# Mixer's head in a four-stage transformer kernel: one convolution tap moved to ScalarE and GpSimd, a logarithm as a polynomial, GpSimd's work in another order

## The reference

```
zxbcdt = LN(x) @ in_proj_w.T                      # z 512, xBC 640, dt 4 columns
dt     = softplus(zxbcdt[..., -4:] + dt_bias)     # 4 heads
xBC    = silu(conv(xBC, 4 taps, causal))          # per channel, along the tokens
xs, B, C = xBC[:512], xBC[512:576], xBC[576:640]
y      = ssd(xs * dt, -exp(A_log) * dt, B, C)     # state-space scan in chunks
y      = (y + xs * D) * silu(z)
x     += (y * rsqrt(mean(y * y) + 1e-5) * norm_w) @ out_proj_w.T
```

## Time and profile before

| | |
|---|---|
| three runs | 520.99, 521.13, 521.2 us, median 521.13 |
| the profiled execution | 521.09 us, of which the span from the first to the last instruction is 519.3 |
| granted TensorE clock, mean | 0.999 of full speed |
| busy: PE, DVE, ACT, POOL | 503.5, 406.6, 313.2, 145.6 us |
| mixer's head, from the first x_resid to the last convolution tap | about 321 to 348.6 us |
| mixer's loop, from decays(0) | about 346 to 402 us |

### The profile page before, as it was taken

The page is one execution under the profiler, slowest core; times in us unless marked ns, Lnnn a source line. Parts: engine busy times, 40 slices in busy tenths (PEclk is TensorE's granted clock), DMA queues, the critical chain, the costliest instruction groups (busy, mean ns, idle before and its releaser), DMA issues.

```text
span 519.3 us, 9035 instructions
## 1 busy us (share of the span) xinstructions
PE 503.5 (97%) x2950; PEld 426.7 (82%) x2951; DVE 406.6 (78%) x895; ACT 313.2 (60%) x784; POOL 145.6 (28%) x285
## 2 busy tenths in 40 slices
PE   6999999999999999999999999989999999999996
PEld 5778899999999988678888888867989768888885
DVE  5736567667666789899999899985888879899777
ACT  4656878688687754574534445899873365344342
POOL 1432434345243320020110111379554020020110
PEclk9999999999999999999999999999999999999999
DMA  7320100000000303100030000000000000000101
GB/s 278 125 81 3 40 2 2 1 1 2 2 2 8 151 2 107 42 1 1 0 141 2 2 0 1 1 2 1 1 2 1 0 1 1 1 0 1 40 2 40
DMA packets 5933, 14.17 MB, mean 27 GB/s; under 512 B 640, under 2 KB 3200, under 8 KB 5888
## 3 DMA queue, kind: packets, MB, share of 16 engines
q1 hardware_dynamic: 5888, 13.60, 7.5%
HBM read 12.55 MB, written 1.05 MB: 26 GB/s over the span
## 4 chain that ended last, share of the span: by engine, by line
PE 79%; DVE 12%; issue 3%; ACT 3%; DMA 1%; POOL 1%; SPq 0%; DVEq 0%; ACTq 0%; POOLq 0%
PE psum L172 61%; PE psum L493 4%; DVE xs L1994 2%; PE psum L525 2%; PE psum L1809 1%; PE psum L241 1%; DMA w_raw<-in_wk 1%; PE psum L1813 1%; PE psum L1819 1%; DVE f_t L1315 1%; DVE ln_stats L214 1%; DVE xn L234 1%; PE psum L1836 1%; PE psum L486 1%; ACT f_sil L1201 1%
## 5 line engine op out<-in xcount | busy, mean ns | idle before, releaser
L172 PE MATMUL psum<-xT_hl,ffn_w_hl 128*128 128x512 f32 x312 | 77.7, 395 | 0.7 <-ACT f_sil L1201 0.6
L172 PE MATMUL psum<-f_um,ffn_w_hl 128*128 128x512 f32 x288 | 72.8, 399 | 1.1 <-DVE f_t L1315 0.6
L172 PEld LDWEIGHTS psum<-xT_hl,ffn_w_hl 128*128 128x128 f32 x312 | 56.2, 188 | 13.1 <-DVE ffn_w_hl L916 1.1
L172 PEld LDWEIGHTS psum<-f_um,ffn_w_hl 128*128 128x128 f32 x288 | 53.1, 188 | 15.0 <-DVE f_um L1327 1.7
L1201 ACT ACTIVATE f_sil<-psum 128x512 f32<-128x512 f32 (+1 forms) x48 | 28.4, 596 | 49.5 <-PE psum L172 49.4
L1225 ACT ACTIVATE f_ch_hl<-f_ch 128x512 fp32r<-128x512 f32 x48 | 30.3, 631 | 41.7 <-DVE f_ch L1384 40.0
L172 PE MATMUL psum<-xT_hl,wq_hl 128*128 128x512 f32 x192 | 52.0, 407 | 0.6 <-ACT qT L593 0.6
L172 PE MATMUL psum<-wo_hl,oT_hl 128*128 128x256 f32 x384 | 50.5, 281 | 1.0 <-DVE oT_hl L726 0.6
L172 PEld LDWEIGHTS psum<-wo_hl,oT_hl 128*128 128x128 f32 x384 | 47.7, 188 | 3.5 <-DVE oT_hl L726 1.1
L593 ACT ACTIVATE qT<-psum 128x512 f32<-128x512 f32 x32 | 35.3, 1104 | 22.6 <-PE psum L172 22.4
L602 ACT ACTIVATE probs<-probs,small 120x66 f32<-120x66 f32 x120 | 39.9, 338 | 8.2 <-DVE small L703 8.2
(11 more groups left out here) (265 smaller groups left out, 1147.6 us busy)
## 6 DMA issues: line engine op xcount, KB each, us to landing
w_raw<-in_wq SPq DMA_DIRECT2D x4, 512.0 KB, 3.9
w_raw<-in_wo SPq DMA_DIRECT2D x4, 512.0 KB, 3.3
ffn_w_raw<-in_ffn SPq DMA_DIRECT2D x3, 576.0 KB, 5.8
ffn_w_raw_far<-in_ffn SPq DMA_DIRECT2D x3, 576.0 KB, 5.4
ssd_w_raw<-in_ssd SPq DMA_DIRECT2D x3, 512.0 KB, 5.3
x_resid<-in_x SPq DMA_DIRECT2D x2, 512.0 KB, 5.2
out_x<-x_resid SPq DMA_DIRECT2D x4, 256.0 KB, 2.1
w_raw<-in_wk SPq DMA_DIRECT2D x1, 512.0 KB, 6.3
```

Of the source, the lines that this page charges most:

```text
L172: i = e.matmul(dst, lhs(a), rhs(b), start=start and n == 0, stop=stop and n == len(TERMS) - 1, **kw)
```

## The change

Three edits in the mixer, and what they bring with them.

One tap of projection 0 leaves VectorE: ScalarE multiplies the whole bank by the farthest tap into a new tile `far` (`far_taps`, behind last_tap(0)), and GpSimd adds it to the result (`far_adds`, behind carries(0), a tensor_tensor of 509 tokens). CV_ORDER loses (0, 3).

The logarithm becomes log(1 + E) = 2 artanh(E / (2 + E)), a polynomial in the square of the ratio: GpSimd runs 15 counted steps in place of 11, and ScalarE no Ln. The cumulative sum moves behind projection 16 on TensorE, the reciprocal ahead of (5, 1) on VectorE, and the copies of the sum behind (7, 2) in place of (6, 2). ScalarE's silu(2), (3) and the later ones stand in another order; ident_r and mask_r are made ahead of GpSimd's steps.

On GpSimd join(1) to join(4) move ahead of the make_xd, join(2) ahead of rhs_col; in the loop make_xd(3) runs in turn 0, and make_xd(6), (7), (8) in turns 1, 2, 3, behind gate.

```diff
-            CV_ORDER = [(0, 1), (0, 2), (0, 3), (1, 1), (1, 2), ...
+            TAP_AT = [FAR + 1] + list(range(FAR + 2, FAR + 1 + NC))
+            CV_ORDER = [(0, 1), (0, 2), (1, 1), (1, 2), ...
@@ pe
-                for n in range(12, 16):
+                for n in range(12, 17):
                     in_proj(e, n)
                 e.wait_ge(S["dt_pool"], DT_DONE)
                 conv_done(e, 4)
...
-                for n in range(16, 2 * NB):
+                for n in range(17, 2 * NB):
                     in_proj(e, n)
@@ act
+                def far_taps():
+                    for n in range(FAR):
+                        tap = PR_CW + n
+                        e.activation(far[:, n, :], bank(IN_BANK[0]), ACT.Copy, scale=par[:, tap:tap + 1]).then_inc(S["tap"], 1)
...
                 last_tap(0)
+                far_taps()
                 dt_copy(1)
...
                 last_tap(12)
-                e.wait_ge(S["dt_pool"], 2)
-                e.activation(L1, U1, ACT.Ln).then_inc(S["dt_act"], 1)
+                silu(2)
                 last_tap(13)
+                silu(3)
                 last_tap(14)
-                silu(2)
+                last_tap(15)
                 silu_z(16)
-                silu(3)
-                last_tap(15)
-                silu_z(17)
                 silu(4)
                 silu(5)
+                silu_z(17)
+                silu(6)
                 silu_z(18)
-                silu(6)
+                silu(7)
                 silu_z(19)
-                for i in range(7, NC):
+                for i in range(8, NC):
                     silu(i)
@@ dve
-                conv((0, 3), (1, 1), (1, 2))
+                conv((1, 1), (1, 2))
...
-                conv((4, 1), (4, 2), (5, 1))
-                e.wait_ge(S["dt_pool"], 5)
-                e.reciprocal(R1, N1).then_inc(S["dt_dve"], 1)
-                conv((4, 3), (5, 2), (6, 1), (5, 3), (6, 2))
+                conv((4, 1), (4, 2))
+                e.wait_ge(S["dt_pool"], 2)
+                e.reciprocal(R1, TWO).then_inc(S["dt_dve"], 1)
+                conv((5, 1), (4, 3), (5, 2), (6, 1), (5, 3), (6, 2), (7, 1), (6, 3), (7, 2))
...
-                conv((7, 1), (6, 3), (7, 2), (8, 1), (7, 3), (8, 2), (9, 1), (8, 3), (9, 2), (9, 3))
+                conv((8, 1), (7, 3), (8, 2), (9, 1), (8, 3), (9, 2), (9, 3))
@@ pool
+                def far_adds():
+                    conv_read(e, 0)
...
+                        e.tensor_tensor(out, far[:, n, 0:HALF - d], out, ALU.add).then_inc(S["gt"], 1)
...
                 carries(0, slice(0, 1), 0)
+                far_adds()
                 carries(1, slice(2, CB), NC // 2 - 1)
...
-                step(e.tensor_scalar(U1, E1, 1.0, None, ALU.add))
-                step(e.tensor_scalar(D1, U1, -1.0, None, ALU.add))
-                step(e.tensor_scalar(Z1, D1, 0.0, None, ALU.is_equal))
-                step(e.tensor_tensor(N1, D1, Z1, ALU.add))
+                step(e.tensor_scalar(TWO, E1, 2.0, None, ALU.add))
                 step(e.tensor_scalar(AN, AN, -1.0, None, ALU.mult))
                 e.wait_ge(S["dt_dve"], 4)
-                step(e.tensor_tensor(SP, R1, E1, ALU.mult))
-                e.wait_ge(S["dt_act"], 3)
-                step(e.tensor_tensor(N1, L1, Z1, ALU.add))
-                step(e.tensor_tensor(SP, N1, SP, ALU.mult))
+                step(e.tensor_tensor(RATIO, E1, R1, ALU.mult))
+                step(e.tensor_tensor(SQ, RATIO, RATIO, ALU.mult))
+                step(e.tensor_scalar(SERIES, SQ, LOG_SERIES[4], LOG_SERIES[3], ALU.mult, ALU.add))
+                for term in LOG_SERIES[2::-1]:
+                    step(e.tensor_tensor(SERIES, SERIES, SQ, ALU.mult))
+                    step(e.tensor_scalar(SERIES, SERIES, term, None, ALU.add))
+                step(e.tensor_tensor(SP, SERIES, RATIO, ALU.mult))
                 step(e.tensor_tensor(DT, SP, RL, ALU.add))
...
                 join(0)
+                join(1)
...
                 select(0)
+                join(2)
                 e.wait_ge(S["rhs"], 1)
                 e.tensor_scalar(rhs_col, f32(rhs_cs), par[:, CS_FIRST:CS_FIRST + 1], None, ALU.mult).then_inc(S["rhs"], 1)
-                join(1)
+                join(3)
+                join(4)
                 make_xd(1)
-                for i in range(2, NH + 1):
-                    join(i)
                 make_xd(2)
-                make_xd(3)
...
-                    if c < NH - 1:
-                        make_xd(NC // 2 + 1 + c)
+                    if c == 0:
+                        make_xd(3)
                     if c >= 1:
                         gate(c - 1)
+                    if 1 <= c < HT:
+                        make_xd(NC // 2 + c)
```

More of the change, by code:

```diff
@@ L1558, in mixer @@
             carry = small[:, 32:32 + CB * (CONV - 1)].rearrange("p (b k) -> p b k", b=CB)
-            V, AV, E1, U1, L1, D1, Z1, N1, R1, SP, DT, DA, RL = (sd[:, 32 * i:32 * i + 32] for i in range(13))
+            V, AV, E1, TWO, RATIO, SQ, SERIES, R1, SP, DT, DA, RL = (sd[:, 32 * i:32 * i + 32] for i in range(12))
             AN, VE, RI = sm[:, 0:4], sm[:, 8:16], sm[:, 16:24]
@@ L1589, in g_part @@
                 return g_last[c][w] if c in LAST else (g_hi, g_lo)[w]
+            FAR = 1
+            far = at("far_taps", [P, FAR, HALF], F32, A_W)
             st_t = at("state_decayed", [P, NH, P], F32, A_W + 30720)[:, :, :]
@@ L1600, in mixer @@
             names = ("xda cs cm rhs mb sel gs da raw wh wl bcz ip tap ipz part join cv sl xd dt dt_dve dt_pool dt_act de L G xt X xdd wt ce Y St st1 st y g ghi glo g2 ss "
-                     "ve ri O fin bt").split()
+                     "ve ri O fin bt gt").split()
             S = {n: sem(f"ssd_{n}") for n in names}
@@ L1606, in mixer @@
             upto = cf[:, C_UPTO:C_UPTO + P]
-            DT_DONE = 11
+            DT_DONE = 15
+            LOG_SERIES = (2.00000001, 0.66666322, 0.40024595, 0.27965158, 0.28157778)
             NB = CB + NH
@@ L1617, in mixer, with conv_read @@
             NC = len(convs)
-            CV_ORDER = [(0, 1), (0, 2), (0, 3), (1, 1), (1, 2), (1, 3), (2, 1), (3, 1), (2, 2), (3, 2), (2, 3), (3, 3),
+            TAP_AT = [FAR + 1] + list(range(FAR + 2, FAR + 1 + NC))
+            CV_ORDER = [(0, 1), (0, 2), (1, 1), (1, 2), (1, 3), (2, 1), (3, 1), (2, 2), (3, 2), (2, 3), (3, 3),
                         (4, 1), (4, 2), (5, 1), (4, 3), (5, 2), (6, 1), (5, 3), (6, 2), (7, 1), (6, 3), (7, 2), (8, 1),
                         (7, 3), (8, 2), (9, 1), (8, 3), (9, 2), (9, 3)]
-            assert len(CV_ORDER) == TAPS * NC
+            assert len(CV_ORDER) == TAPS * NC - FAR and len(TAP_AT) == NC
             def cv_at(i, tap):
                 return CV_ORDER.index((i, tap)) + 1
+            def conv_read(e, i):
+                e.wait_ge(S["cv"], cv_at(i, TAPS if i else TAPS - FAR))
             def conv_done(e, i):
-                e.wait_ge(S["cv"], cv_at(i, TAPS))
+                if i:
+                    conv_read(e, i)
+                else:
+                    e.wait_ge(S["gt"], FAR)
             def bank_taken(e, n):
                 if n in convs:
-                    conv_done(e, convs.index(n))
+                    conv_read(e, convs.index(n))
                 else:
@@ L1990, in conv @@
                         tap = par[:, PR_CW + CONV * b + CONV - 1 - d:PR_CW + CONV * b + CONV - d]
-                        e.wait_ge(S["tap"], i + 1)
+                        e.wait_ge(S["tap"], TAP_AT[i])
                         if d > 1:
@@ L2130, in carries @@
                 def carries(n, tiles, last):
-                    e.wait_ge(S["tap"], last + 1)
+                    e.wait_ge(S["tap"], TAP_AT[last])
                     b0, nb = tiles.start, tiles.stop - tiles.start
@@ L2144, in carries @@
                                     ALU.add).then_inc(S["part"], 1)
+                def far_adds():
+                    conv_read(e, 0)
+                    for n in range(FAR):
+                        d = TAPS - n
+                        out = cb_pre[:, d:HALF]
+                        if n:
+                            e.wait_ge(S["gt"], n)
+                        e.tensor_tensor(out, far[:, n, 0:HALF - d], out, ALU.add).then_inc(S["gt"], 1)
                 carries(0, slice(0, 1), 0)
+                far_adds()
                 carries(1, slice(2, CB), NC // 2 - 1)
@@ L2169, in join @@
                     e.tensor_tensor(out, out, carry[:, b, :], ALU.add).then_inc(S["join"], 1)
+                e.wait_ge(S["wl"], len(WL_ORDER))
+                e.wait_ge(S["ip"], 12)
+                e.tensor_copy(ident_r, ident)
+                e.tensor_scalar(mask_r, repeat(upto, NH), -1.0, -MASKED, ALU.add, ALU.mult).then_inc(S["mb"], 1)
                 e.wait_ge(S["dt_dve"], 3)
@@ L2173, in pool @@
                 e.wait_ge(S["dt_act"], 2)
-                step(e.tensor_scalar(U1, E1, 1.0, None, ALU.add))
-                step(e.tensor_scalar(D1, U1, -1.0, None, ALU.add))
```

(14 more changed lines are left out.)

## The result

The changed kernel takes 522.6 us (median of 9, 522.51 to 523.12) against 521.13 (9 runs, 520.97 to 521.26): a ratio of 1.0031, 95% interval 1.0022 to 1.0040. It is slower, by 1.47 us or 0.3%, and the interval leaves out 1; 522.9 was forecast. Its profiled execution took 523.12 (span 521.3), the slowest of the nine, because everything ahead of the mixer came 0.47 later in it.

The account below looks back on a forecast made before the run. Bounds: VectorE's taps in the head, then at tile 4 two equal chains, TensorE's and the loop VectorE, GpSimd, VectorE. -0.42 + 0.47 + 0.25 + 1.57 = +1.87 on 521.09 gave 522.96, taken as 522.9; range 521.5 to 523.9.

Parts of the forecast that it names:

- Head, -0.42: Before the loop: with one tap fewer on VectorE, the loop starts 0.42 us earlier.
- the head gains nothing: Rival: fillers and rhs_col, or one of GpSimd's 15 steps, take the 0.42; 523.4 us, chance 0.12.
- Turn 1, +0.47: Loop turn 1: make_xd(6) behind gate(0) delays select(3), so decays(3) on TensorE comes 0.47 us later.
- Contention, +0.25: Loop turn 2: xdd(3), moved by make_xd(7), runs over VectorE's g_lo(1) and lengthens it by 0.25 us.
- Turn 3, +1.57: Loop turn 3: make_xd(8) stands between gate(2) and inverse_rms(0), for which VectorE's final(0) waits; 1.57 us later.
- The forecast's own low end, 522.3: Lower end of the forecast's own range, for no contention and the head gaining the full 0.66 us.
- the loop isn't a bound: Rival: TensorE's own chain bounds the loop, its waits absorb VectorE's delay, head's gain stays; 520.7 us, chance 0.09.
- The scaling is short in its new place: Rival: in the loop a scaling takes 0.62 us and select(3) isn't late; 521.6 us, chance 0.04.
- The two engines lock each other out fully: Rival: g_lo(1) waits for the end of xdd(3), 1.0 in place of 0.25; 523.7 us, chance 0.04.

Follow-up runs that it names:

- e7: e1 with tap 3 of projection 0 back on VectorE (no far tap on ScalarE and GpSimd): 521.15 us.
- e4: Changed kernel with only make_xd(6) ahead of gate, make_xd(7) and (8) still behind: 522.35 us.
- e2: Kernel before the change with make_xd(8) alone moved, from ahead of gate(1) to behind gate(2): 522.68 us.
- e5: Changed kernel with inverse_rms(0), (1), (2) one turn earlier, ahead of gate; scalings still behind gate: 521.21 us.
- e12: Changed kernel with each make_xd adding 0.0, then multiplying by D from the tile: 521.53 us.
- e6: Changed kernel with make_xd multiplying by the number 1.0 in place of D from a tile: 522.6 us.
- e1: Changed kernel with make_xd(6), (7), (8) all ahead of gate in the same turns: 521.04 us.
- e11: e1 with make_xd(1), (2), (3) and (6) in four other instruction forms: 520.73 us.
- e8: e1 with inverse_rms(0), (1), (2) one turn earlier, ahead of gate: 520.83 us.

## Why the prediction was right

The three large terms of the sum were right in their cause and nearly in their size; the fourth, the contention, was wrong in both, and luck kept that small. On the clock behind x_resid:

- **Head, -0.42.** Measured -0.36 (w_mix 30.35 against 30.71), by e7's trace all of it the tap's. ScalarE bounded the low parts as written (0.21 of wait). a_rep gave TensorE its wait of 0.29, as the 0.27 before, through an extra projection. decays(0) ended at 349.13 on the clock of before, past the 349.0 that was to decide for the rival "the head gains nothing", and the rival still fell: the load for decays(1) came 0.36 earlier (353.20 - 321.44 against 353.09 - 320.97), as the exponential did. But the fillers now run up to it with no gap, where 0.11 us were free before, so another tap less on VectorE need not bring anything. The far tap's addition took 1.44 on GpSimd, not 1.29, and ended at 328.56 ahead of silu(0) at 329.58: hidden.
- **Turn 1, +0.47.** The load for decays(3) comes at 361.39 - 321.44 = 39.95, before at 360.80 - 320.97 = 39.83: +0.12 in all, so +0.48 for the turn. e4 gives 0.25 by the medians and 0.5 by the trace. A second path came out as late, unforeseen: g_lo(0) took 1.43 in place of 0.94 beside the moved xdd(2), and VectorE, 0.38 early at its start, began with_skip(1) 0.12 late. The chain that ended last runs through TensorE and ScalarE there; e4 moves both and can't tell them apart.
- **Contention, +0.25.** This term was put in the wrong place. with_skip(2) is later by +0.14 in all, so it was worth 0.02. xdd(3) did not move by about 1 us but by 1.5 and more, since make_xd(7) now follows gate(1), and g_lo(1) met select(4) instead. That took 0.96 in place of 0.43, and VectorE lost nothing (0.71). TensorE did: its load for decays(4) waited 0.76 us for select(4) and came 0.65 later (368.01 - 321.44 against 366.89 - 320.97), hidden by the longer delay of turn 3. The price was wrong as well as the place. In every trace in which g_lo starts while an xdd still has 0.2 us or more to go, it ends 0.54 to 0.56 behind xdd; in the kernel before too, where g_lo(0) starts 0.68 into xdd(2) and has only 0.38 of it to wait for:

```profile
360.70 1.06 POOL L2235 TENSOR_TENSOR x_dt_decay<-x_dt,decay 128x512 f32<-128x512 f32 x1
```

So 0.94 was not the price of a meeting but of its last third. Had xdd(3) run from 366.4 to 367.4 as predicted, g_lo(1) would by this have ended near 367.95 and lost about 0.8 us, an estimate, and not 0.25. That it cost 0.02 is luck.
- **Turn 3, +1.57.** Measured 1.54 (inverse_rms(0) +1.68 in all, of which 0.14 came with it). e2 has it alone: 1.57. e5 shows its path, e12 that it goes with the length of the scaling.
- **Behind it.** At tile 4 the product L1847 starts at 388.56 - 321.44 = 67.12, before at 65.46: +1.66, and L940 +1.65. VectorE's loop had no time to give back: it is slower than TensorE, not equal to it. In the kernel before, final comes every 6.06 us (371.23, 377.29, 383.34, 389.39), TensorE's turn in between is 5.75 (L1775 at 367.48, 373.23, 378.97 in its chain), and TensorE looks like the bound only because it starts the loop ahead and is caught up with at tile 4. Predicted was +1.87; the contention's 0.23 is nearly the whole error inside the mixer; the head's gain was put 0.06 too high and turn 3's loss 0.03. The medians stand 0.18 lower than that. Half of it may be f1's (from L940 to its last group of products 113.28 us here and 113.37 before); the rest I can't tell from the spread of single executions. The forecast's own low end, 522.3, does not follow from its terms: without the contention and with the full 0.66 they give 522.47.

Of the rivals, "the loop isn't a bound" fell by e2. "The scaling is short in its new place" fell by the trace, 1.56 in all six; but its counterpart, a scaling that is short by its form, exists, and e12 priced it as the rival did (521.53 against 521.6). The Trainium skill, page "GPSIMD Engine Reference", section "Elementwise — side-by-side cycle accounting", gave 768 ns for 512 elements in a tight loop. The trace doesn't agree for the form that the line uses (1.49 to 1.57), and the pair of operations is shorter than that figure (0.62 to 0.69), as the mask with 0.62 already was. My reason, that the factor is read from a tile, was wrong: e6 and e12 show the factor to be worth 0.07. "The two engines lock each other out fully" was set aside by a wrong reading of the row of 0.94. Beside an xdd VectorE does stand still until xdd has ended: g_lo(0) here starts at 361.47, xdd(2) ends at 362.35, g_lo(0) at 362.90, 0.74 longer than its 0.69 alone. The rival's time did not come because g_lo(1) met no xdd. Beside a scaling the lock is not for its whole length: in e1 g_lo(1) ended 0.3 ahead of the scaling that it met.

## What to carry to other kernels

An engine that is 28% busy can still set the time: ask of each of its instructions who waits for the one behind it. The free time of such an engine lies in front of its own waits; work that nobody is in a hurry for belongs there, ahead of the wait and not behind it. And compare the turns and not the busy shares: the loop over VectorE and GpSimd takes 6.06 us a tile and TensorE, the busiest engine, 5.75. So 1.57 us put into that loop is 1.57 us at the end.

## What the runs showed of the hardware

- GpSimd's tensor_scalar on 512 float32 columns takes 1.49 with one operation (multiply or add, by a number), 1.56 by a scalar from a tile, and 0.62 or 0.69 with the pair add, multiply. Why one operation is dearer than two is open.
- GpSimd's xdd (two inputs, 1.05 us) locks out VectorE's subtraction of two SBUF tiles (g_lo, 0.69 alone) for as long as it runs. When g_lo starts inside an xdd with 0.2 us or more to go, it ends 0.54 to 0.56 behind xdd's end, in all fourteen traces: 0.34 of xdd left and 0.89 long, 0.59 and 1.13, 0.75 and 1.30, 0.88 and 1.43. Each of g_lo(2) to (4) pays 0.2 this way in the kernel before.
- The other way round GpSimd waits. A scaling that starts 0.35 us into g_lo takes 2.01 in place of 1.56 and ends 1.42 behind g_lo's end (before); select(4), starting with g_lo(1), takes 0.96 in place of 0.43 (changed kernel).
- A scaling under way holds g_lo up only in its first part. g_lo ended 1.23 us behind the scaling's start where it started 0.01 ahead of it or 0.36 into it (1.24 long in e1, 0.87 in e11), though the scaling lasts 1.55; 0.53 into it, g_lo took 0.71 (e11).
- With starts 0.01 to 0.02 us apart and an xdd just ending, either of them went first: in e1 and e7 VectorE paid 0.55 (1.24) and the scaling nothing (1.55), in e8 GpSimd paid 0.54 (2.10) and g_lo nothing (0.69). What decides it is open. The Trainium skill, page "SBUF — State Buffer", section "Who interferes with whom", names these two kinds of instruction as contending, and calls the shared ports an exclusive lock. The traces agree for xdd and for GpSimd behind g_lo; beside a scaling of 1.55, which g_lo(1) outran in e1 (367.48 against 367.80), they don't.
